# Score steps of the first layer moved into its side projections, and a later gather of the second layer

## The reference

```python
u = jnp.einsum('bid,bjd->bij', h, h) / temper          # scores, temper = sqrt(384)
a = jax.nn.softmax(u, axis=-1)
delta = a * adjacency_matrix
attn = delta / (jnp.sum(delta, axis=-1, keepdims=True) + 1e-10)
hl = h @ wl.T + b_l                                    # upper side
hs = h @ ws.T + b_s                                    # self
hr = h @ wr.T + b_r                                    # lower side
ctx = einsum('bij,bjd->bid', attn * upper, hl) + diag_a[..., None] * hs + einsum('bij,bjd->bid', attn * lower, hr)
h = relu((ctx - mean) / jnp.sqrt(var + 1e-12) * g + beta)
```

## Time and profile before

| | |
|---|---|
| median of three runs | 1624.32 us (1623.67 to 1625.14) |
| the profiled execution's own time | 1624.36 us |
| its span from the first to the last instruction | 1622.6 us |
| TensorE matmul | 1604.5 us busy, 99% |
| TensorE weight load | 1579.7 us, 97% |
| VectorE | 1397.6 us, 86% |
| ScalarE | 1079.5 us, 67% |
| GpSimd | 1294.3 us, 80% |
| granted TensorE clock | 0.998 of full |

### The profile page before, as it was taken

One profiled execution on the slowest core, in us unless ns is written; L12 is line 12 of the kernel. 1 busy time (PEld: TensorE's weight loads), 2 busy tenths in 40 slices (PEclk: granted clock), 3 DMA queues, 4 the chain that ended last, 5 costly groups with the idle time before them and its releaser, 6 DMA issues.

```text
span 1622.6 us, 35792 instructions
## 1 busy us (share of the span) xinstructions
PE 1604.5 (99%) x9267; PEld 1579.7 (97%) x9267; DVE 1397.6 (86%) x4490; ACT 1079.5 (67%) x2958; POOL 1294.3 (80%) x1665
## 2 busy tenths in 40 slices
PE   9999999999999999999999999999999999999996
PEld 8999999999999999999999999999999999999995
DVE  7888888888888888888888888888888888888887
ACT  6666666666666666666666666666666666666665
POOL 6788888888878888888888888888888888888874
PEclk9999999999999999999999999999999999999999
DMA  5555555555555555555555555555555555555541
GB/s 184 124 138 130 132 128 139 127 132 128 139 126 133 129 137 126 134 134 131 131 130 133 131 134 128 134 132 134 128 137 130 132 128 139 127 133 129 133 107 49
DMA packets 589175, 211.28 MB, mean 130 GB/s; under 512 B 473952, under 2 KB 572256, under 8 KB 589152
## 3 DMA queue, kind: packets, MB, share of 16 engines
q1 hardware_dynamic: 490752, 198.91, 47.5%
q10 hardware_dynamic: 98400, 12.11, 4.8%
HBM read 128.98 MB, written 81.92 MB: 130 GB/s over the span
## 4 chain that ended last, share of the span: by engine, by line
PE 96%; POOL 1%; DVE 1%; ACT 1%; issue 1%; DMA 0%; ACTq 0%; DVEq 0%; SPq 0%; POOLq 0%
PE p_proj L464 73%; PE p_gather L584 17%; PE p_score L458 5%; POOL proj_split L299 0%; DMA w_raw<-WT 0%; POOL w L1340 0%; POOL rstd L1293 0%; ACT proj_split L1053 0%; DMA rows_mem<-rows_blocks 0%; POOL attnT_split L1289 0%; DVE proj L758 0%; ACT spread L1112 0%; DVE p_gather L716 0%; ACT p_score L1030 0%; DVE p_gather L724 0%
## 5 line engine op out<-in xcount | busy, mean ns | idle before, releaser
L464 PE MATMUL p_proj<-w,hT_layer 128*128 128x384 f32 x6912 | 1352.5, 339 | 0.0
L464 PEld LDWEIGHTS p_proj<-w,hT_layer 128*128 128x128 f32 x6912 | 1221.7, 188 | 0.2
L299 POOL TENSOR_TENSOR proj_split<-proj,proj_split 128x768 fp32r<-128x768 f32 x253 | 467.2, 1846 | 88.1 <-ACT proj_split L1053 88.1
L584 PE MATMUL p_gather<-proj_split,attnT_split 128*128 128x384 f32 x1536 | 324.0, 345 | 1.8 <-issue 1.5
L758 DVE TENSOR_TENSOR proj<-p_proj,bias_all 128x768 f32<-128x768 f32 x256 | 243.8, 952 | 79.1 <-PE p_proj L464 79.0
L1289 POOL TENSOR_TENSOR attnT_split<-attnT,attnT_split 128x256 fp32r<-128x256 f32 x256 | 189.8, 741 | 152.3 <-ACT attnT_split L1044 152.2
L584 PEld LDWEIGHTS p_gather<-proj_split,attnT_split 128*128 128x128 f32 x1536 | 264.7, 188 | 23.3 <-POOL attnT_split L1289 21.2
L1293 POOL TENSOR_TENSOR rstd<-veps,neg_half 128x1 f32<-128x1 f32 x384 | 209.5, 549 | 56.3 <-DVE veps L702 40.7
L1053 ACT ACTIVATE proj_split<-proj 128x768 fp32r<-128x768 f32 x256 | 213.0, 832 | 5.2 <-DVE proj L758 4.2
L458 PE MATMUL p_score<-hT_layer 128*128 128x256 f32 x768 | 215.2, 281 | 1.1 <-DVE hT_layer L745 0.8
L1057 ACT ACTIVATE normed<-gathered,nbias,rstd 128x384 f32<-128x384 f32 x128 | 90.7, 709 | 140.3 <-POOL nbias L1297 140.3
(11 more groups left out here) (69 smaller groups left out, 1677.7 us busy)
## 6 DMA issues: line engine op xcount, KB each, us to landing
swap_mem<-blocks SPq DMA_DIRECT2D x124, 256.0 KB, 2.2
whole<-swap_mem SPq DMA_DIRECT2D x496, 64.0 KB, 2.5
xt_raw<-xT SPq DMA_DIRECT2D x128, 192.0 KB, 2.8
xn<-x SPq DMA_DIRECT2D x128, 192.0 KB, 2.7
out<-o SPq DMA_DIRECT2D x128, 192.0 KB, 2.0
rows_mem<-rows_blocks SPq DMA_DIRECT2D x123, 192.0 KB, 1.9
adj_layer<-adj SPq DMA_DIRECT2D x256, 64.0 KB, 2.1
rowsT<-rows_mem SPq DMA_DIRECT2D x246, 48.0 KB, 2.6
```

Source lines behind the costliest of these rows:

```text
L299: op.tensor_tensor(proj_split[u][:, LO], proj[u][:, UP:LOW + 1, :], proj_split[u][:, HI].bitcast(F32), ALU.subtract).then_inc(s_proj_lo[k], 1)
L464: return nc.tensor.matmul(p_proj[:, which, 0:D], hT_of(k, b)[:, slot, st, c, :], w[:, k, which, mv, c, :], start=(n == 0), stop=(n == 8))
L584: last = nc.tensor.matmul(home(k, b)[:, 0:D], AT_split[u][:, st, side, :], proj_split[u][:, mv, side, :], start=(side == UP and n == 0), s ...
```

## The change

TensorE's stream alone is changed. `pair_slice` is replaced by two functions. `score_early` places the three score steps of layer 1 for graph i+2 behind steps 1, 3 and 5 of the sides of layer 1 for graph i; its first step waits for `s_lo` and then `s_kept` (with the count of the iteration before). `score_late` places the three score steps of layer 2 for graph i-2 behind steps 0, 1 and 2 of the self part of layer 1. The gather of layer 2 comes after nine steps of the sides of layer 2 instead of seven. The number of instructions of each kind is the same.

```diff
-            def pair_slice(b0, slot0, b1, slot1, n):
-                if n == 2:
-                    if isinstance(b1, int) and b1 == 2:
+            def score_early(b0, slot0, chunk):
+                if chunk == 0:
+                    done(pe, s_lo[0], b0)
+                    if isinstance(b0, int) and b0 == 6:
                         done(pe, s_negmax[0], 5)
                         done(pe, s_negmax[1], 1)
                     else:
+                        done(pe, s_kept, b0 - 7)
+                step = score_step(0, b0, slot0, chunk)
+                if chunk == C - 1:
+                    step.then_inc(s_parts[0], 1)
+
+            def score_late(b1, slot1, n):
+                if n == 0:
+                    done(pe, s_lo[1], b1)
+                    if not isinstance(b1, int) or b1 > 2:
                         done(pe, s_kept, b1 - 3)
-                    if b0 is not None:
-                        done(pe, s_lo[0], b0)
-                if b0 is not None and 2 <= n < 2 + C:
-                    step = score_step(0, b0, slot0, n - 2)
-                    if n == 1 + C:
-                        step.then_inc(s_parts[0], 1)
-                if n == 2 + C:
-                    done(pe, s_lo[1], b1)
-                if 2 + C <= n < 2 + 2 * C:
-                    step = score_step(1, b1, slot1, n - 2 - C)
-                    if n == 1 + 2 * C:
+                if n < C:
+                    step = score_step(1, b1, slot1, n)
+                    if n == C - 1:
                         step.then_inc(s_parts[1], 1)
...
+                    if early is not None and n in (1, 3, 5):
+                        score_early(*early, n // 2)
...
-                    b0 = i + 2 if live(i, i + 2) else None
-                    project_sides(0, i, r, 1, i - 4, range(18))
-                    project_self(0, i, r, 1, i - 4, pair=(b0, (r + 2) % 4, i - 2, p))
-                    project_sides(1, i - 3, q, 0, i, range(7))
+                    early = (i + 2, (r + 2) % 4) if live(i, i + 2) else None
+                    project_sides(0, i, r, 1, i - 4, range(18), early=early)
+                    project_self(0, i, r, 1, i - 4, late=(i - 2, p))
+                    project_sides(1, i - 3, q, 0, i, range(9))
                     gather(1, i - 4)
-                    project_sides(1, i - 3, q, 0, i, range(7, 18))
+                    project_sides(1, i - 3, q, 0, i, range(9, 18))
                     project_self(1, i - 3, q, 0, i)
                     gather(0, i, True)
```

More of the change, by code:

```diff
@@ L493, in pair_slice, with project_sides @@
                     else:
-                        done(pe, s_kept, b1 - 3)
-                    if b0 is not None:
-                        done(pe, s_lo[0], b0)
-                if b0 is not None and 2 <= n < 2 + C:
-                    step = score_step(0, b0, slot0, n - 2)
-                    if n == 1 + C:
-                        step.then_inc(s_parts[0], 1)
-                if n == 2 + C:
-                    done(pe, s_lo[1], b1)
-                if 2 + C <= n < 2 + 2 * C:
-                    step = score_step(1, b1, slot1, n - 2 - C)
-                    if n == 1 + 2 * C:
+                        done(pe, s_kept, b0 - 7)
[6 more added lines that the diff above has]
+                    if not isinstance(b1, int) or b1 > 2:
+                        done(pe, s_kept, b1 - 3)
+                if n < C:
+                    step = score_step(1, b1, slot1, n)
+                    if n == C - 1:
                         step.then_inc(s_parts[1], 1)
-            def project_sides(k, b, slot, before, b_last, steps, scored=None, first=0, last_part=14):
+            def project_sides(k, b, slot, before, b_last, steps, scored=None, first=0, last_part=14,
+                              early=None):
                 if 0 in steps:
@@ L523, in project_sides, with project_self @@
                     last.then_inc(s_proj[k], 1)
-            def project_self(k, b, slot, before, b_last, scored=None, first=0, last_part=8, pair=None):
+            def project_self(k, b, slot, before, b_last, scored=None, first=0, last_part=8, late=None):
                 done(pe, s_self_biased[before], b_last)
@@ L530, in project_self @@
                     last = project_step(k, b, slot, SELF, n)
-                    if pair is not None:
-                        pair_slice(*pair, n)
+                    if late is not None:
+                        score_late(*late, n)
                     if scored is not None and n < 8:
```

## The result

| | before | changed |
|---|---|---|
| median | 1624.43 us (6 runs, 1623.67 to 1625.42) | 1635.6 us (6 runs, 1634.52 to 1636.88) |
| profiled execution | 1624.36 us | 1636.18 us |
| its span | 1622.6 us | 1634.5 us |

The ratio is 1.0068, with a 95% interval of 1.0055 to 1.0081: the changed kernel is slower by 11.2 us. The lines of the changed kernel stand five lower than before from the gather on: L589 is the gather (before L584), L750 `low_rows` (L745), L763 the bias of the sides (L758), L1294 `low_sides` (L1289), L1324 `low_input` (L1319), L1298 the roots (L1293).

The account below looks back on a forecast made before the run. TensorE, busy 99%, was taken as the bound. Loop terms 9.01 + 0.07 + 0.11 + 3.01 + 0.38 gave 12.58 us, 0.134 more an iteration; 1624.36 + 16.1 = 1640.4 us, 8-in-10 range 1623 to 1652.

Parts of the forecast that it names:

- The start: TensorE bounds the kernel, busy 99%; 0.12 us an iteration idle at the gather, 14.6 us in all to win.
- edit 2: Gather of layer 2 two side steps later: its wait for L1289 stays (3.54 against 3.53 us of work before it), worth 0.
- Edit 1: Layer 1's three score steps moved into the sides: the sides' end, and all following L758, come 0.36 us later.
- Edit 3: Layer 2's score steps moved to self-part steps 0 to 2: L745's result has 0.42 us cover, cost 0.
- The moved wait: First layer 1 score step's wait for L1319: cover goes from 0.22 to -0.14 us, loop of 12.58 us against 12.446.
- L758 to L1319 9.01: Loop term from L758's start on VectorE to L1319's end on GpSimd: 9.01 us, taken as rigid.
- the start of the load 0.07: Loop term from L1319's end to the score step's weight load: 0.07 us, ends 0.05 and 0.17.
- the way from the score step to the last side step: Loop term on TensorE: 3 score and 15 side steps, 0.36 + 15 x 0.1765 = 3.01 us.
- B: Rival: the early wait for L1319 is met in time, no change, 1624.4 us; chance 0.15.
- C: Rival: the gather's wait goes and no other comes, faster, 1609.8 us; chance 0.10.
- D: Rival: score steps behind the early wait issue every 0.176 us, not 0.12; 1662 us, half of it 1651; chance 0.13.

Follow-up runs that it names:

- edit 2 alone: Kernel before with only the gather of layer 2 moved, after nine side steps instead of seven; 1607.82 us, ratio 0.9897.
- The last experiment: Changed kernel with `low_input` put ahead of the output's root and bias on GpSimd; 1701.32 us, ratio 1.0472.
- the kernels with one step more and one less in it: Changed kernel with layer 1's score steps behind side steps 0, 2, 4 (1656.28 us) or 2, 4, 6 (1623.15 us) instead of 1, 3, 5.
- the memsets: GpSimd column memsets ahead of `low_input`: one (1639.87 us) or four (1651.39 us) on the changed kernel, one on the kernel before (1625.73 us).
- edit 2 undone: Changed kernel with the gather of layer 2 after seven side steps again, score steps as changed; 1662.48 us, ratio 1.0237.
- both covers given back: Changed kernel with layer 1's score steps behind side steps 5, 7, 9 and layer 2's gather after eleven; 1608.67 us, ratio 0.9898.

## Why the prediction was right, and where it was off

**The start: TensorE is the bound and 0.12 us an iteration is idle.** Right; edit 2 alone took that idle time away, 16.5 us where 14.6 were reckoned. The sum of the steps set beside it (12.34) takes 0.176 us for every step, which not every stretch has, so it is the gather's 0.12 us that carries this.

**Edit 1 shifts all that hangs on L758.** Right in kind: `low_input` ends at 810.36, 0.36 us after the iteration's start at 810.00, where it ended 0.04 us before that start. These 0.40 us aren't the forecast 0.36 alone. The sides' end is also held up by the new wait (0.17), while the side steps are 0.05 shorter in sum and the next start is 0.10 further off; that makes 0.38.

**Edit 2 pays back what edit 1 takes from the gather.** Right, and shown from both sides: undone it costs 27 us, alone it brings 16.5. "Worth 0" is true of the gather's wait under both edits together, not of edit 2 by itself. The gather's loads wait 20.5 us, near the 21 forecast. The view puts only 10.8 of it on `low_sides`; most of the rest are waits too short for it to name a releaser.

**Edit 3 costs 0.** Right (1.0005). The cover was reckoned at 0.42 us; in the changed kernel `low_rows` ends at 812.61 + 0.56 = 813.17 and the load starts at 813.66, 0.49 later. The last experiment used it up and paid for it.

```profile
812.61 0.56 DVE L750 TENSOR_TENSOR hT_layer<-p_rows,hT_layer 128x384 fp32r<-128x384 f32 x1
```

```profile
813.66 0.19 PEld L458 LDWEIGHTS p_score<-hT_layer 128*128 128x128 f32 x1
```

**The moved wait closes a loop.** Right: shown by the kernels with one step more and one less in it and by the memsets, against the kernel before, where one memset is free. Its terms: L758 to L1319 9.01 (9.01 in the iteration walked above); the start of the load 0.07. Here I was right by luck: I thought that the wait on `s_lo` would be on an instruction of its own in every iteration. In the rows above the load starts 0.05 us after `low_input` in one iteration (810.36 to 810.41) and 0.12 in another (797.78 to 797.90); the trace shows 0.05 in three of the four unrolled copies and 0.12 in the fourth, mean 0.07.

The Trainium skill's "Perfetto Trace Analysis", section "Identifying Dependency Chains", lets a wait go to an EventSemaphore in front, but doesn't say which of several does. The 0.05 us are those of a load that waits itself; that the order of the code decides was my reading, and it fell.

**The term that was mis-sized is the way from the score step to the last side step, 3.01 us.** It measured 0.12 + 2.85 = 2.97 (810.64 to 813.49, and the score step's 0.12). The side steps behind the early score steps are (2.42 - 0.34)/12 = 0.1733 us apart, and I had taken 0.1765 from steps that no score step had preceded. The term is 3.0075 - 2.97 = 0.0375 us too long, 4.5 us in 120 iterations. With it put right the sum is 16.1 - 4.5 = 11.6 us; the profiled executions differ by 11.8, the medians by 11.2.

The signs that the prediction named are there: an iteration of 12.544 us (12.58 forecast), L763's wait 88.6 us (95), the new wait 20.7 + 7.0 = 27.7 us, of which a little is from the filling of the pipeline (24). The wait takes more than the iteration grows. Of the 0.22 us that the weight load waits in an iteration (row 810.41) TensorE's matmuls lose the 0.17 read above, the shorter steps give 0.05 back and the gather's wait 0.02 ((23.3 - 20.5)/120), which leaves the 0.10.

**The rivals.** B (no change) falls: the wait was there, 0.22 us in the iteration shown. The 64 deep queue of the Trainium skill's "TensorE: Matmul & The Clock Gate", section "What happens when you issue a matmul", didn't hide it: TensorE's loads stood idle until 0.05 us after `low_input` ended. C (faster) falls here, and is what edit 2 does alone. D (dear score steps behind the wait) falls: they take 0.12 us.

## What to carry to other kernels

A wait that is moved towards its producer has to be priced as a loop: if the producer hangs on something that the consumer releases later in the same iteration, every step of the bound engine between wait and release counts in full (0.172 us for a step of 0.173 here), and a shift of one piece takes cover from all that hang on its end. Before moving a consumer to win back a wait, count the work of the bound engine from the event that starts the chain, not from where the iteration begins. And an experiment that reorders one engine's queue has to be followed through every queue that waits for it.

## What the runs showed of the hardware

The distance of projection steps of the same shape isn't one number. With TensorE's clock granted at 0.998 of full speed (the 2.4 GHz level) in the kernel before and in the changed one, it is about 0.176 us in some stretches and 0.173 in others, which last for some eight to twenty steps and change at score steps and gathers. It isn't the wait that does it: in the kernel with edit 2 undone the early score step doesn't wait, and the thirteen steps behind (822.58, below) are as close.

```profile
822.58 2.42 PE L464 MATMUL p_proj<-w,hT_layer 128*128 128x384 f32 x13
```

Behind score steps with two projection steps between each the distance was 0.173, behind three score steps in strict alternation 0.176 in the changed kernel; spreading the latter, in the kernel with both covers given back, gave 5.2 us. But behind the six alternating ones of the kernel before, eight steps took 1.55 us, (1.55 - 0.34)/7 = 0.173 too. So the rule isn't simply the alternation; what sets the distance stays open. Of the 3 us more that edit 2 alone brought it may explain a part; that wasn't tested.

The Trainium skill's "TensorE: Matmul & The Clock Gate", section "Wait — 56ns, not 53.3ns?", has N / 2.4 GHz + 2.5 ns from start to start for N columns; an estimate from it is 162.5 ns for 384 columns. Neither distance of this kernel agrees with it, and the measured ones, 173 and 176 ns, decide.

Small GpSimd instructions overlap: memsets of a column are recorded with 0.10 us each, but four in a row started 0.03 us apart (815.84, 815.87), and a single one put the start of `low_input` back by only 0.04 us (0.14 to 0.18 after the bias's start). Why isn't shown.
